# Six exp buffers instead of seven, and a softmax tail one key tile later, in an eight-core attention and LoRA-FFN block

## The reference

```
x = x + LN(ATTN(LN(x)))
x = x + LN(FFN(LN(x)))
```

## Time and profile before

| what | value |
|---|---|
| median of the 2 runs shown | 851.43 us (821.81 and 881.04) |
| the profiled execution, its own time | 821.57 us |
| its span on the slowest core (core 0) | 820.0 us |
| spans of the eight cores | 812.0 to 820.0 us |
| mean granted TensorE clock of the cores | 0.864 to 0.877 |

### The profile page before, as it was taken

How to read it: one execution, slowest core, us unless ns; L and a number is a source line. 1 busy time by engine, 2 the same in 40 slices (tenths; PEclk the granted TensorE clock), 3 DMA queues, 4 the chain that set the end, 5 groups by cost and what they waited for, 6 DMA issues and landing times.

```text
span 820.0 us, 9701 instructions; the slowest of 8 cores (812.0 to 820.0 us)
## 1 busy us (share of the span) xinstructions
PE 602.1 (73%) x3056; PEld 282.4 (34%) x3056; DVE 412.6 (50%) x694; ACT 404.8 (49%) x585; POOL 40.8 (5%) x67
## 2 busy tenths in 40 slices
PE   0356576649888888888988887954742549999991
PEld 0244454413333333333333332321212434444440
DVE  1555656344444444444444441575886751534533
ACT  0577777528888888888788885021313210000000
POOL 5400000010000000000000001100000000000000
PEclk9965656559999999999999999986985869999996
DMA  8932331079700000000000000995444000233231
GB/s 175 227 126 103 131 127 52 0 108 166 139 1 1 1 1 1 1 1 0 1 1 1 0 1 6 209 224 205 154 185 173 2 11 17 104 154 153 103 154 51
DMA packets 15585, 67.02 MB, mean 82 GB/s; under 512 B 5800, under 2 KB 5808, under 8 KB 9392
## 3 DMA queue, kind: packets, MB, share of 16 engines
q0 software_dynamic: 10624, 32.85, 18.0%
q1 hardware_dynamic: 4912, 33.56, 11.6%
HBM read 65.70 MB, written 16.78 MB: 101 GB/s over the span
## 4 chain that ended last, share of the span: by engine, by line
PE 47%; DVE 23%; ACT 10%; DMA 9%; issue 8%; DVEq 1%; ACTq 0%; POOL 0%; POOLq 0%; SPq 0%
PE psF L1029 14%; PE psO L627 6%; PE psO L630 6%; PE psS L641 5%; PE psS L644 4%; DMA xmid<-xre 3%; DMA wqkva_b<-wqkva 3%; DVE woL L614 2%; DVE recB L611 2%; ACT den_r L674 2%; DVE xre L798 2%; DVE st6b L754 2%; DVE st6c L806 2%; ACT lnb L343 2%; DVE psW L765 2%
## 5 line engine op out<-in xcount | busy, mean ns | idle before, releaser
L649 ACT ACTIVATE eS<-psS 128x1024 bf16<-128x1024 f32 x256 | 247.0, 1022 | 53.4 <-PE psS L644 51.8
L1029 PE MATMUL psF<-Wt,lnT 128*128 128x512 bf16 x512 | 114.6, 385 | 0.7 <-DVE xaT L948 0.7
L641 PE MATMUL psS<-QX,cT 128*128 128x512 bf16 x256 | 99.1, 387 | 12.6 <-ACT eS L649 10.7
L627 PE MATMUL psO<-eS,V 128*65 128x512 bf16 x256 | 97.3, 380 | 5.1 <-DVE woL L614 5.1
L644 PE MATMUL psS<-QX,cT 128*128 128x512 bf16 x256 | 99.1, 387 | 0.0
L630 PE MATMUL psO<-eS,V 128*65 128x512 bf16 x256 | 97.1, 379 | 0.0
L785 PE MATMUL psW<-wo_b,woL 128*128 128x512 bf16 x256 | 66.7, 427 | 35.1 <-DVE xre L798 31.5
L759 ACT ACTIVATE rstdb<-mvb,eps_b 128x1 f32<-128x1 f32 x16 | 4.7, 295 | 154.3 <-DVE mvb L757 135.7
L363 PE MATMUL psP<-ident_b,lnb 128*128 128x128 bf16 x256 | 30.7, 287 | 62.9 <-ACT slab L371 32.3
L1029 PEld LDWEIGHTS psF<-Wt,lnT 128*128 128x128 bf16 x512 | 50.0, 99 | 64.4 <-issue 7.4
L754 DVE BATCH_NORM_STATS2 st6b<-psF 128x6 f32<-128x512 f32 x32 | 19.9, 685 | 69.4 <-PE psF L1045 69.4
(11 more groups left out here) (124 smaller groups left out, 743.1 us busy)
## 6 DMA issues: line engine op xcount, KB each, us to landing
xtmp<-x_full SPq DMA_DIRECT2D x16, 1024.0 KB, 5.3
Wt<-wt POOLq DMA_DIRECT2D x16, 512.0 KB, 25.9
xre<-x_full SPq DMA_DIRECT2D x8, 1024.0 KB, 5.6
xmid<-xre POOLq DMA_DIRECT2D x8, 1024.0 KB, 4.2
xre<-xmid SPq DMA_DIRECT2D x8, 1024.0 KB, 4.8
out<-xre POOLq DMA_DIRECT2D x8, 1024.0 KB, 4.1
wo_b<-wo POOLq DMA_DIRECT2D x1, 4096.0 KB, 31.0
wqkva_b<-wqkva POOLq DMA_DIRECT2D x1, 768.0 KB, 22.8
```

The source lines that it names most:

```text
L627: e.matmul(psO[0:65, 0:512], Vsb[kt][:, h * 65:(h + 1) * 65], eS[kb][:, 0:512], start=(kt == 0), stop=(kt == RT_F - 1), skip_group_check=True)
L641: e.matmul(psS[ks][:, 0:512], cT[:, kt * 128:(kt + 1) * 128], QX[hb][:, 0:512], start=True, stop=True)
L649: lambda e, kb=kb, ks=ks: e.activation(eS[kb][:, :], psS[ks][:, 0:1024], AF.Exp, scale=SCALE))
L1029: inst = e.matmul(psF[qb][:, c * 512:(c + 1) * 512], lnT2[q][:, t * 128:(t + 1) * 128], Wt_sb[t][:, c * 512:(c + 1) * 512], start=(t == 0) ...
```

## The change

Three numbers and three places in the emission order. `dx` and `dwp` get six semaphores each instead of seven, so a DMA waits for the one six places before it. Of the `rstd` tiles only indices 0 to 5 were ever used; the seventh goes. eS has six buffers. In each head nothing of AV is emitted before kt 6; there AV0 and AV1 are emitted together, behind S6 and ahead of exp 6, which writes eS[0]; from kt 7 on AV(kt-5) follows as before. The three pieces of the former head's tail are emitted at kt 1, 2 and 3 instead of 0, 1 and 2.

```diff
-DMA_POOLS = {"dx": [f"dx{i}" for i in range(7)],
-             "dwp": [f"dwp{i}" for i in range(7)],
+DMA_POOLS = {"dx": [f"dx{i}" for i in range(6)],
+             "dwp": [f"dwp{i}" for i in range(6)],
...
-            rstd = [E1(nc.sbuf_tensor(f"rstd{i}", [128, 1], F32)) for i in range(7)]
+            rstd = [E1(nc.sbuf_tensor(f"rstd{i}", [128, 1], F32)) for i in range(6)]
...
-            eS = [E2(nc.sbuf_tensor(f"eS{i}", [128, NQ], BF16)) for i in range(7)]
+            eS = [E2(nc.sbuf_tensor(f"eS{i}", [128, NQ], BF16)) for i in range(6)]
...
                 def emit_av(kt):
-                    kb = kt % 7
+                    kb = kt % 6
...
                 for kt in range(RT_F):
-                    kb = kt % 7
+                    kb = kt % 6
...
                     P.run("pe", [B("cT"), qxB], [B(f"psS{ks}")], mmS)
+                    if kt == 6:
+                        emit_av(0)
+                        emit_av(1)
                     P.run("act", [B(f"psS{ks}")], [B(f"eS{kb}")],
...
                     if h > 0:
-                        if kt == 0:
+                        if kt == 1:
                             head_den(h - 1)
-                        elif kt == 1:
+                        elif kt == 2:
                             head_tail_a(h - 1)
-                        elif kt == 2:
+                        elif kt == 3:
                             head_tail_b(h - 1)
-                    if kt >= 5:
+                    if kt >= 7:
                         emit_av(kt - 5)
```

## The result

| | before | after |
|---|---|---|
| median | 821.73 us (10 runs) | 831.35 us (11 runs, 828.92 to 832.5) |
| profiled execution: own time, span of the slowest core | 821.57, 820.0 | 828.41, 826.9 |
| ratio, 95% interval | | 1.0113 [1.0097, 1.0130] |

The changed kernel is slower by 9.3 us (8.0 to 10.7): 821.73 x 0.0113. The forecast of 828.0 had the direction and nearly all of the mechanism, but its 6.4 us are too small, and 831.35 lies above the 826 to 831 that it gave itself. The profiled execution is the fastest of the changed kernel, 2.9 us under the median.

A forecast was written before the change was run, and what follows sets the result against it. Attention was taken as bound by the den_r-to-AV0 chain and PE's work from AV0 to S7. 821.57 + 6.4 (15 x 0.40 = 6.0, head 0 0.4) + 0 (clock) + 0 (semaphores) = 828.0 us; own range 826 to 831, with rivals 822 to 836.

The forecast's parts named there:

- The tail, one key tile later: Attention head boundary: L596 and L605 wait behind S2 and S3, so AV0 starts 0.83 us later, at 6.98.
- S6 ahead of AV0: Attention: S6 runs in PE's wait for woL, taking 0.43 off AV0 to S7; net 0.40 us later per head.
- The added wait: Attention: exp 6 must wait for AV0, starting at 7.68 instead of 7.27; nothing else before AV6 waits for it.
- Head 0: First attention head, no tail to wait for: AV0 behind S6 puts 0.43 more between S6 and S7; 0.4 us.
- The clock: Attention boundaries: granted clock falls at two of 15 inner boundaries again, no change; bounds -0.9 to +5.6 us.
- Six semaphores: Start: wqkva issued 6.5 us later but hidden behind ident's queue; taken as 0, at most 6.5 us.
- Phase 3: agw and xmid issued later, xmid by 1.9 us, but DMA engines are full; taken as 0, at most 2.9.
- A: Rival, attention: the clock falls at nearly every boundary, +5.6 us on top of 6.4, 833.6 us; chance 0.08.
- B: Rival, start: wqkva lands late and 6.5 us pass to L389 and through phase 1, 834.5 us; chance 0.07.
- C: Rival, attention: S1 in den_r's hole puts PE 0.43 ahead in each of 15 heads, 815.1 us; chance 0.04.
- D: Rival, attention: nothing shows because the tail was hidden anyway, 821.6 us; chance 0.05.
- the limits: Outcome chances: up to 838.0 us counts as same; A and B together, or B with half the clock falls (840.1), slower: 0.06.

The follow-up runs named there:

- e3: Kernel before with only the tail moved to kt 1, 2, 3; seven eS buffers, AV from kt 5, seven semaphores: 849.34 us, ratio 1.0363.
- e2: Kernel before with only six eS buffers and the first two AVs held until after S6; tail and seven semaphores kept: 821.17 us, ratio 0.9994.
- e4: Changed kernel with seven semaphores again in dx and dwp: 828.96 us, ratio 1.0100.
- e1: Kernel before with only six semaphores each in dx and dwp: 822.54 us, ratio 1.0012.
- e9: Kernel before, seven semaphores, with wqkva issued right behind ident, ahead of ones, sel and brow: 822.74 us, ratio 1.0005.
- e6: Changed kernel with L605 directly behind L596 at kt 2, ahead of S3: 845.71 us in a single run.
- e7: e3 plus five idle matmuls per head boundary in PE's waits, results unused: 847.63 us, ratio 1.0298.
- e5: Changed kernel with L596 directly behind L583 at kt 1 and L605 at kt 2, ahead of S3: 823.61 us, ratio 1.0016.
- e11: e8 with AVs two tiles behind S instead of three: 816.74 us, ratio 0.9926 against the kernel before.
- e8: Kernel before, but DVE copies psO out right behind the last AV, woL uses the copy, AVs run three tiles behind: 808.05 us, ratio 0.9822.

## Why the prediction fell short, and what it had right

The steps that failed are sizes, and the mechanism held. The tail's sum has "S3 starts at 3.13 to 3.16 and issues for 0.43. L605 starts at 3.56", and from this 0.40 us a head; L605 came at +3.65 and the price is 0.48. This lies above the prediction's own bound of 0.43: attention took 15 x 0.48 + 0.43 = 7.6 us more, and the bounds were 3.6 to 6.9. The second is the term for six semaphores, taken at 0 and measured at 1 us.

- **The tail, one key tile later: right, 0.1 short.** L583 at +1.16, S2 ahead of L596, S3 ahead of L605, the old distances behind: all seen. The working put L605 one issue step (0.22) behind S3's second matmul; it came 0.31 behind. From there on everything is 0.1 late, and the period is 20.94 for 20.86. This is the first mis-sized term: 15 x 0.08 = 1.2 us. The trace of the kernel before had this gap at the same place, in lines that the earlier trace rows leave out, and the working did not use them (core 0; L596 follows at 261.56, L605 at 262.33):

```profile
261.25 0.38 PE L644 MATMUL psS<-QX,cT 128*128 128x512 bf16 x1
...
262.02 0.38 PE L644 MATMUL psS<-QX,cT 128*128 128x512 bf16 x1
```

- **S6 ahead of AV0: right.** S6 runs within the wait for woL, its 0.43 leave the stretch from AV0 to S7: 1.60 forecast, 271.04 to 272.64 measured. In e3, without it, the same tail costs 0.92 a head instead of 0.48.
- **The added wait: right, and free.** exp 6 is released by L630 at +7.75; e2, with this wait and the hold alone, is no slower. exp 4 starts 0.35 later than its row of exps, which was not foreseen and moved nothing.
- **Head 0: the 0.43 was right** (19.61 on cores 2 and 6).
- **The clock: taken at 0, right in number, and by luck.** Inner falls are two on every core after, as forecast, at 0.4 to 0.6 (three cores of the kernel before had none, the others two). Nothing in the working says why it should stay at two: e3, which has the same order up to the place where the clock falls, has nine. And the sum counted inner boundaries alone. Head 0 had no term; in the profiled execution it begins at half clock on six cores, which is 0.9 us. That this belongs to the change is not shown: e4, with the same attention, had it in full on one core, and e1, with attention as it was, on three.
- **Six semaphores: taken at 0, measured 1 us** (e1, and after against e4, neither clear of noise). The argument on the start held: on core 3 6.1 us of later issue were hidden behind the queue, and e9 shows the issue time to be worth nothing. (It took ident's landing from PE's idle time, 25.7; ident landed at 25.5, so the misreading did no harm.) What the argument did not reach is attention: 0.36 of the 1 us is the head in which woL starts late, and that head comes with six semaphores (see the end). The rest may be later landings, but the first L389's scatter by as much from core to core and run to run, with six and with seven.
- **Phase 3: right.** agw and xmid go out later relative to their tiles, at no cost.
- **The sum.** 6.4 forecast; 1.2 + 1.0 more (the odd head's 0.36 is in the 1.0) gives 8.6, and with head 0's clock 9.5. Both lie within the measured 8.0 to 10.7, so the runs do not tell whether the 0.9 belongs there.
- **The rivals.** A (clock at most boundaries) did not happen in the changed kernel, but e3, e6 and e7 show its falls, and e3 and e7 at a higher price than was worked out (1.5 to 1.8 us a fall instead of 0.43). Given how near it lay, the chance was given for a wrong reason: the fill in den_r's hole was not what kept it away, since e3 has that as well. B's price was nearly all hidden: wqkva landed 0.7 later on core 3. Its sign, a first L389 at 38 or later, was seen on four cores, but the kernel before has one at 38.1 and e9 one at 40.1, so the sign tells nothing. C is refuted: with S1 in the hole and L605 at +2.73 (e5) the head takes 20.39, a gain of 0.07, not 0.43, and e2 has the same 20.39 without S1 in the hole. That PE is 0.43 ahead is worth nothing while S6 waits for exp 4 and AV0 stands behind it. D (no change) lies outside the interval, which begins at 1.0097.
- **A slip in the limits.** The 840.1 there is A and B together; B with half the clock falls would be 837.3, under the 838.0.

## What to carry to other kernels

Where a chain crosses engines (here den_r, L583, reciprocal, L596, rec8, L605, recB, woL), ask of each link on an in-order engine what stands ahead of it and what that waits for; a link moved one step later pays for the waits of its new neighbours, and a neighbour pushed behind a link pays too (e6, e11). Filling a wait that ends a chain gains nothing; take what is waited for off the chain, as the copy of psO does. And after any reordering look at the granted clock per head: e4 and e3, which differ in the hold alone, lost about 1 us and 16 us by it.

## What the runs showed that was not expected

- **How often the clock falls depends on small things of the order.** By core, none or 2 of 15 boundaries before, 2 on every core after, 7 or 9 with e3, 9 or 12 with e6, 2 to 4 with e8, 1 to 7 in e11. A fall costs 0.4 to 0.6 where most of it lies in a stretch in which PE waits anyway, 1.5 to 1.8 where AVs run in it. The Trainium skill (TensorE: Matmul & The Clock Gate, A second HAM failure mode: psum-queue depth-cycling) describes such swings; e3, with nine of 15, agrees with it, the kernel before and the changed one, with none or two, hardly.
- **L596, L605 and L549 come 0.1 us late behind a wide matmul**: 0.31 from the start of the second matmul of S or AV to theirs (266.39 and 266.70, 267.31 and 267.62, 271.68 and 271.99), where S and AV follow each other in 0.215. It is so in the kernel before as well; why is not shown.
- **One head is 0.36 us longer on all eight cores, at the same place, and it comes with the six semaphores.** woL starts 0.46 after recB instead of 0.1, with nothing in the trace that it waits for (DVE's timeline, changed kernel, core 3):

```profile
480.45 1.22 DVE L614 TENSOR_TENSOR woL<-psO,recB 64x1024 bf16<-64x1024 f32 x1 [0.46 <-DVE recB L611]
```

  The same 0.46 stands ahead of the same woL, that of head 13, in all four kernels with six semaphores (the changed one, e1, e5, e6) and in none of the nine with seven. In e5 and e6 it lies in slack; e1 and the changed kernel pay 0.36. So it is part of what the semaphores cost. By what way they delay an instruction of DVE is open.
